# Cross attention of a two-layer decoder: projections and output product as three rounded products, their weights fetched and split piece by piece

## The reference

```python
q = (x @ Wq).reshape(B, Sq, 16, 128)          # x: 512 x 512,   Wq: 512 x 2048
k = (ctx @ Wk).reshape(B, Skv, 16, 128)       # ctx: 512 x 256, Wk: 256 x 2048
v = (ctx @ Wv).reshape(B, Skv, 16, 128)
q = rmsnorm(q, gq); k = rmsnorm(k, gk)
scores = einsum('bqhd,bkhd->bhqk', q, k) / sqrt(128)
out = einsum('bhqk,bkhd->bqhd', softmax(scores), v)
out = out.reshape(B, Sq, 2048) @ Wo           # Wo: 2048 x 512
```

## Time and profile before

| | us |
|---|---|
| median of 3 runs | 2998.81 (2998.12 to 3002.98) |
| profiled execution | 3006.79 |
| its span, first to last instruction | 3005.1 |
| TensorE busy | 2727.0, 91% |
| VectorE busy | 1975.9, 66% |
| ScalarE busy | 1100.2, 37% |
| GpSimd busy | 633.0, 21% |

### The profile page before, as it was taken

The page is one execution under the profiler, slowest core; times in us unless marked ns, Lnnn a source line. Parts: engine busy times, 40 slices in busy tenths (PEclk is TensorE's granted clock), DMA queues, the critical chain, the costliest instruction groups (busy, mean ns, idle before and its releaser), DMA issues.

```text
span 3005.1 us, 28723 instructions
## 1 busy us (share of the span) xinstructions
PE 2727.0 (91%) x8882; PEld 1493.1 (50%) x8882; DVE 1975.9 (66%) x3923; ACT 1100.2 (37%) x1999; POOL 633.0 (21%) x569
## 2 busy tenths in 40 slices
PE   6887887888869988899999999999999999899998
PEld 2333333333337845455545555455545555488886
DVE  3896996997996547688836787378826887323332
ACT  4335335335333322255514554155514454121111
POOL 0542543533520136411101110111101110000000
PEclk9998988998989989999999999999999999999999
DMA  3111111111130213200021001200011002400000
GB/s 118 49 56 44 63 43 54 60 49 50 61 114 29 77 43 139 80 15 18 15 58 51 18 15 31 79 18 15 19 58 49 17 15 80 141 7 28 29 15 14
DMA packets 67406, 145.34 MB, mean 48 GB/s; under 512 B 8115, under 2 KB 24755, under 8 KB 66230
## 3 DMA queue, kind: packets, MB, share of 16 engines
q1 hardware_dynamic: 58134, 111.40, 11.2%
q0 software_dynamic: 5472, 21.01, 1.8%
q10 hardware_dynamic: 3648, 11.08, 1.1%
HBM read 113.77 MB, written 29.69 MB: 48 GB/s over the span
## 4 chain that ended last, share of the span: by engine, by line
PE 64%; DVE 16%; issue 10%; POOL 5%; ACT 2%; DMA 1%; SPq 1%; DVEq 0%; POOLq 0%; ACTq 0%
PE bank L492 34%; PE bank L834 7%; POOL h L1603 3%; PE bank L789 3%; DVE h L1266 3%; PE bank L848 3%; PE bank L849 3%; PE bank L852 3%; DVE sm L1526 2%; DVE p L1537 1%; DVE val L1465 1%; PE bank L877 1%; PE bank L878 1%; PE bank L774 1%; PE bank L879 1%
## 5 line engine op out<-in xcount | busy, mean ns | idle before, releaser
L1603 POOL TENSOR_TENSOR h<-du,Bb 128x1024 f32<-128x1024 f32 x128 | 300.4, 2350 | 212.7 <-DVE h L1271 163.0
L1266 DVE TENSOR_TENSOR_SCAN h<-bank,h 128x512 f32<-128x512 f32 x256 | 297.8, 1203 | 33.6 <-ACT bank L967 18.3
L967 ACT ACTIVATE bank<-dt,A 128x512 f32<-128x512 f32 x256 | 174.9, 690 | 310.1 <-DVE h L1266 309.9
L1112 ACT ACTIVATE p<-bank,sm,rq 128x512 f32<-128x512 f32 x256 | 199.1, 778 | 210.1 <-DVE sm L1530 210.1
L492 PE MATMUL bank<-pT,v 128*128 128x512 f32 x512 | 234.7, 602 | 3.0 <-ACT pT L904 3.0
L834 PE MATMUL bank<-woh,oT 128*128 128x512 f32 x512 | 226.0, 603 | 10.8 <-DMA woh<-in_Wo 8.8
L492 PE MATMUL bank<-xT,wxq 128*128 128x512 f32 x512 | 230.6, 593 | 3.2 <-ACT xT L904 3.2
L1678 POOL TENSOR_TENSOR rq<-rq,mhalf 128x4 f32<-128x4 f32 x64 | 65.6, 1025 | 791.0 <-DVE rq L1517 791.0
L209 POOL TENSOR_SCALAR rstd<-mv 128x1 f32<-128x1 f32 x96 | 25.4, 265 | 979.8 <-DVE mv L203 979.8
L492 PE MATMUL bank<-kr,q 128*128 128x512 f32 x512 | 230.6, 593 | 0.0
L1526 DVE TENSOR_REDUCE sm<-bank 128x1 f32<-128x512 f32 x256 | 175.3, 685 | 33.9 <-PE bank L492 33.7
(11 more groups left out here) (203 smaller groups left out, 5109.9 us busy)
## 6 DMA issues: line engine op xcount, KB each, us to landing
Bb<-bc_dram SPq DMA_DIRECT2D x32, 512.0 KB, 3.6
Cb<-bc_dram SPq DMA_DIRECT2D x32, 512.0 KB, 3.8
x_dram<-xo POOLq DMA_DIRECT2D x16, 1024.0 KB, 4.7
xc<-x_dram SPq DMA_DIRECT2D x16, 1024.0 KB, 5.3
woh<-in_Wo SPq DMA_DIRECT2D x64, 256.0 KB, 2.7
idx<-in_idx SPq DMA_DIRECT2D x64, 129.0 KB, 2.1
w_dram<-val SPq DMA_DIRECT2D x64, 129.0 KB, 2.5
xc<-in_x SPq DMA_DIRECT2D x4, 1024.0 KB, 7.4
```

The costliest lines, as they stand in the source:

```text
L967: act.activation(bank[2 + n][:, :], dt[:, et, :], ACT.Exp, scale=A[:, et, 2 * w + n:2 * w + n + 1]).then_inc(dA_ready, 1)
L1112: act.activation(p4[:, t, :], bank[4 + t][:, :], ACT.Exp, bias=sm4[:, 4 + t:5 + t], scale=rq[:, hh % 2, 1, t:t + 1], accum_out=sm4[:, 8 + ...
L1266: dve.tensor_tensor_scan(h[:, s, n, :], bank[2 + n][:, :], h[:, s, n, :], 0.0, ALU.mult, ALU.add).then_inc(scanned, 1)
L1603: pool.tensor_tensor(h[:, U % HR, :, :], du[:, et:et + 1, :].to_broadcast([P, 2, S]), Bb[:, w % 2, :, :], ALU.mult).then_inc(dBu_ready, 1)
```

## The change

All four linear products of stage 3 (keys, values, queries, and the output product of sequences 0 to 2) become three rounded products each. The context, x, the weights and the attended values are split into hi and lo. ScalarE rounds; GpSimd subtracts for the three projection weights; VectorE subtracts for the context, x, the attended values and the `Wo` slices. The weights are no longer loaded whole: `Wq` comes per head (128 columns, two buffers), `Wk` and `Wv` per group of four heads (512 columns, one buffer each), again in each sequence. GpSimd's part of the stage is written out for every sequence instead of running in a loop. In stage 0 the keys take the same form as the queries (two Relu passes and an exponential on ScalarE, a plain sum of two SBUF tiles on VectorE), and `key_consumed` is gone. The last sequence keeps its output product in float32.

```diff
-    def key_consumed(j):
-        pe.wait_ge(qk_ready, START + after(c, KD + NT, KD + j + 1))
...
+    dst = qp[:, j, :] if j < KD else kp[:, j - KD, :]
+    dve.tensor_tensor(dst, er[:, j % 2, 0, :], er[:, j % 2, 1, :], ALU.add).then_inc(qk_ready, 1)
...
-    weights(3, wxq, io["Wq"]); weights(3, wxk, io["Wk"]); weights(3, wxv, io["Wv"])
+    load_ctx(0)
+    load_wxk(0)
+    load_wxv(0)
+    load_wxq(0)
+    load_wxq(1)
...
@@ SyncE, in each head @@
+    if after(c, XH, hh + 2) < B * XH:
+        load_wxq(after(c, XH, hh + 2))
+    if hh % 4 == 3 and after(c, GROUPS, hh // 4 + 2) < B * GROUPS:
+        load_wxv(after(c, GROUPS, hh // 4 + 2))
+        load_wxk(after(c, GROUPS, hh // 4 + 2))
...
@@ TensorE @@
     def queries(hh):
+        pe.wait_ge(wxq_split, START + after(c, XH, hh + 1))
+        pe.wait_ge(x3_split, START + after(c, KD, KD))
         d = bank4("q", hh)
-        group(d[:, :], [(wxq[:, k, hh * P:(hh + 1) * P], xT[:, k, :]) for k in range(KD)], a_full)
+        three4(d[:, :], [p for k in range(KD) for p in (
+            (wxq_hi[:, hh % 2, k, :], x_hi3[:, k, :]), (wxq_lo[:, hh % 2, k, :], x_hi3[:, k, :]),
+            (wxq_hi[:, hh % 2, k, :], x_lo3[:, k, :]))], a_full)
...
@@ output product, c < B - 1 @@
+    pe.wait_ge(o_split, START + after(c, XH, hh + 1))
+    for t in range(NT):
+        tt = slice(t * P, (t + 1) * P)
+        pe.matmul(bank[4 + t][:, :], o_hi3[:, hh % 2, tt], w_hi3[:, hh % 2, :], start=(hh == 0), stop=False)
+        pe.matmul(bank[4 + t][:, :], o_hi3[:, hh % 2, tt], w_lo3[:, hh % 2, :], start=False, stop=False)
+        m = pe.matmul(bank[4 + t][:, :], o_lo3[:, hh % 2, tt], w_hi3[:, hh % 2, :], start=False, stop=(hh == XH - 1))
...
@@ ScalarE, in each head, behind oT(hh-1) @@
+    if after(c, XH, hh + 2) < B * XH:
+        round_wxq(after(c, XH, hh + 2))
+    if hh % 4 == 0 and after(c, GROUPS, hh // 4 + 1) < B * GROUPS:
+        round_wxv(after(c, GROUPS, hh // 4 + 1))
+    if hh % 4 == 1 and after(c, GROUPS, hh // 4 + 1) < B * GROUPS:
+        round_wxk(after(c, GROUPS, hh // 4 + 1))
...
+    def round_out(hh):
+        act.wait_ge(wo_loaded[hh % 2], START + 16 * after(c, XH // 2, hh // 2 + 1))
+        if hh >= 2:
+            act.wait_ge(wo_used, START + after(c, XH - 1, hh - 1))
+        act.wait_ge(a_done, START + A0[3] + after(c, PER_A[3], TILES4["o", hh] + 1))
+        act.activation(o_hi3[:, hh % 2, :], oT[:, hh, :], ACT.Copy)
+        act.activation(w_hi3[:, hh % 2, :], woh[:, hh % 2, :], ACT.Copy).then_inc(o_rounded, 1)
...
@@ VectorE @@
+    def out_rest(hh):
+        dve.wait_ge(o_rounded, START + after(c, XH, hh + 1))
+        dve.tensor_tensor(o_lo3[:, hh % 2, :], oT[:, hh, :], o_hi3[:, hh % 2, :], ALU.subtract)
+        dve.tensor_tensor(w_lo3[:, hh % 2, :], woh[:, hh % 2, :], w_hi3[:, hh % 2, :], ALU.subtract).then_inc(o_split, 1)
...
     key_norms(0)
+    x3_rest()
     key_scale(0)
...
@@ at the end of head 12, c < B - 1 @@
+    ctx_rest(c + 1)
...
@@ GpSimd @@
+def wxq_rest(n):
+    pool.wait_ge(wxq_rounded, START + n + 1)
+    pool.tensor_tensor(wxq_lo[:, n % 2, :, :], wxq[:, n % 2, :, :], wxq_hi[:, n % 2, :, :], ALU.subtract).then_inc(wxq_split, 1)
```

More of the change, by code:

```diff
@@ L743, in bank4, with three4 @@
                             return bank[k % 3]
+                        def three4(dst, pairs, inc):
+                            for n, (l, r) in enumerate(pairs):
+                                m = pe.matmul(dst, l, r, start=(n == 0), stop=(n == len(pairs) - 1))
+                            m.then_inc(inc, 1)
                         def ready4(*name):
@@ L801, in _ @@
                         for k in range(KD):
+                            if k == 3:
+                                pe.wait_ge(x3_split, START + after(c, KD, 1))
                             d = bank4("x", k)
@@ L1117, in _ @@
                         for k in range(KD):
-                            bring(xT[:, k, :], got("x", k))
+                            bring(x_hi3[:, k, :], got("x", k))
                         queries(0)
@@ L1134, in _ @@
                                 keys(hh // 4 + 1)
+                            if hh == 12 and c + 1 < B:
+                                round_ctx(c + 1)
+                        if c < B - 1:
+                            round_out(0)
+                            round_out(1)
                         bring(oT[:, XH - 1, :], got("o", XH - 1))
+                        if c < B - 1:
+                            for hh in range(2, XH):
+                                round_out(hh)
             if stages >= 5:
@@ L1517, in query_mean, with ctx_rest, x3_rest @@
                             dve.tensor_scalar(rq[:, hh % 2, 0, :], bank[3][:, 0:4], 1.0 / XD, LN_EPS, ALU.mult, ALU.add).then_inc(rq_raw, 1)
+                        def ctx_rest(n):
+                            dve.wait_ge(ctx_rounded, START + n + 1)
+                            dve.tensor_tensor(ctx_lo[:, :, :], ctx4[:, :, :], ctx_hi[:, :, :], ALU.subtract).then_inc(ctx_split, 1)
+                        def x3_rest():
+                            for k in range(KD):
+                                dve.wait_ge(a_done, START + A0[3] + after(c, PER_A[3], TILES4["x", k] + 1))
+                                dve.tensor_tensor(x_lo3[:, k, :], bank[TILES4["x", k] % 3][:, :], x_hi3[:, k, :], ALU.subtract).then_inc(x3_split, 1)
+                        def out_rest(hh):
+                            dve.wait_ge(o_rounded, START + after(c, XH, hh + 1))
+                            dve.tensor_tensor(o_lo3[:, hh % 2, :], oT[:, hh, :], o_hi3[:, hh % 2, :], ALU.subtract)
+                            dve.tensor_tensor(w_lo3[:, hh % 2, :], woh[:, hh % 2, :], w_hi3[:, hh % 2, :], ALU.subtract).then_inc(o_split, 1)
+                        if c == 0:
+                            ctx_rest(0)
                         key_norms(0)
+                        x3_rest()
                         key_scale(0)
@@ L1544, in _ @@
                                 key_norms(hh // 4 + 1)
+                            if hh == 12 and c + 1 < B:
+                                ctx_rest(c + 1)
+                        if c < B - 1:
+                            for hh in range(XH):
+                                out_rest(hh)
                         if c == B - 1 and stages >= 5:
@@ L1663, in _ @@
                     continue
+                if n == 3:
+                    for c in range(B):
+                        cross(c)
+                    continue
                 with pool.Fori(0, B // 2) as i:
```

161 lines of the change are left out of this document (118 added, 43 removed).

## The result

The changed kernel takes 3006.4 us (median of 10 runs, 3002.7 to 3016.9) against 2998.15 us for the kernel before (10 runs, 2995.9 to 3003.0). The ratio is 1.0032, with a 95% interval from 1.0023 to 1.0040: slower by 0.3%, where 2961 us was forecast. The profiled execution took 3006.47 us with a span of 3004.8; that of before had taken 3006.79, by chance 8.6 above its own median, so the two traces are equally long and can be compared stretch by stretch. One stretch of a trace is good to a few us only: the same code behind the last head's first selection takes 467.3 to 472.5 us over the traces of this case.

The account below looks back on a forecast made before the run. TensorE was taken to lead in the groups, VectorE's look-up in the last four heads, TensorE alone in the output product. The terms summed to -38.1 us, giving 2961 us from the median 2998.81, range 2930 to 3002.

Parts of the forecast that it names:

- GpSimd against VectorE: Stage 3 heads: GpSimd's weight subtractions partly block VectorE, 2 us per group and 3 in the last four heads: +33 us.
- L1465 stretched at all: Sign of a wrong forecast: the look-up's eight selections, expected to be free, lengthen, so their window is no shelter.
- Rival 2: Stage 3: GpSimd blocks VectorE in full, +116, sum +45, 3044 us; sign turns at 61%; chance 0.1 for anything above break-even.
- Rival 4: VectorE bounds the groups too, which stay at 67.6 us; only the output product gains: 2996 us, chance 0.05.
- The groups: Stage 3, 12 groups of four heads: each takes 63.3 us instead of 67.6, together -51.6 us.
- The last four heads: End of each sequence: stay at VectorE's 13.29 us per head, plus ctx_rest in three sequences: +4.2 us.
- The output product: Three sequences: 45.6 us each, first product 1.1 later, so 8.5 less each: -25.5 us.
- The boundary: Between sequences, three times: VectorE's x parts eat the keys' and values' 2.65, about 0.9 stays: -2.7 us in all.
- The start of stage 3: First keys wait for the rests of context and keys, 1258.9 us at best instead of 1251.64: +6.5 us.
- Stage 0: Without key_consumed TensorE starts about 1.3 us earlier; between -2.1 and +2.3 per sequence, taken as -2 over four.
- The sum: All terms: -51.6 + 4.2 - 25.5 - 2.7 + 6.5 - 2 + 33 = -38.1 us.
- Rival 3: TensorE's granted clock drops to 1.2 GHz in places of stage 3: about +25, 2986 us, chance 0.1.

Follow-up runs that it names:

- experiment 7: Kernel before plus one GpSimd subtraction per head, the eight selections taking constants for their two table columns: 3114.2 us; with 128x1024 subtractions 3019.1 us, ratio 1.0074.
- experiment 5: Changed kernel with the three weights' subtractions cut to 4 columns per slice after the first ones, results wrong: 2931.7 us, ratio 0.9768.
- experiment 8: GpSimd subtraction moved right behind the head's inverse root, beside the row maxima: added to the kernel before 3005.9 us; in the changed kernel 2972.9 us.

## Why the prediction was wrong, point by point

- **The step that failed: GpSimd against VectorE, +33.** It assumed: "So they seem to read one port at the plain rate, as the scans do, and I expect them to be free." The selections were the worst hit of all, +86 us (258.0 against 171.6); "L1465 stretched at all" had been named as a sign of being wrong. The step compared 0.35 us with the masks' 0.25 at one length and took the difference for a plain pace. By the rows in experiment 7 it is a fixed part of some 120 ns. And the earlier trace rows held the counter-example: L1287 is itself a `tensor_scalar` with a column (in PSUM), and it was held. The look-up grew by 112 us, three quarters of the 151 that all 92 subtractions come to by the prediction's own lengths, and the kernel lost 75 (experiment 5): the term was 42 too small.
- **Rival 2** had the right mechanism and too high a time (3044): it put 116 on the path, and 75 fell there. That is 65%, just past its break-even of 61%.
- **Rival 4** foretold that a group stays at 67.6, and it did (68.2 against 67.9), but by the hold of rival 2 and not by VectorE's own work. Its sum is wrong: -38 without the groups' -51.6 is +13.5, not -3, so 3012 and not 2996.
- **The groups, -51.6**: measured +4.3. With the subtractions cut away it is 12 x (64.2 - 67.9) = -44, with them on VectorE -33. So the walk through the group was about right (64.2 against 63.3); what failed was the step above.
- **The last four heads, +4.2**: +28.3, of which +2.9 is left without the subtractions. VectorE has no slack there, as the earlier trace rows said, and each held microsecond counts fully: the look-ups there are 25.2 us longer than before, and the heads 25.4 longer than with the subtractions cut away.
- **The output product, -25.5**: -25.9 by itself. 45.4 to 48.4 a sequence against 45.6. Right.
- **The boundary, -2.7**: product and boundary together were to give -28.2 and gave -19.6; with the subtractions cut away -20.0. Over three boundaries the changed kernel's product starts 2.3 later and is 25.3 shorter. From the first keys to the first query it takes +0.2, and from there to the first selection +3.3. The waits for `x_lo` eat the matmuls' 2.65, as the prediction had read it:

```profile
PE bank L792 <- DVE x_lo L1638: 6.5, 4, 1.6
PE bank L867 <- DVE x_lo L1638: 6.2, 4, 1.9
```

  The +3.3 is TensorE's clock. In the kernel with the rests cut away, the queries behind the first of these boundaries run at a granted clock of 1.00 (2.4 GHz), those behind the third at 0.50 (1.2 GHz):

```profile
1575.00:1578.00 3.00, 2.97 (x14) 2.42 (x15) 2.50 (x4) 0.00 (x0) 0.13 (x1) 1.00 0.02 5
2216.00:2219.00 3.00, 3.00 (x8) 2.32 (x8) 2.33 (x4) 0.00 (x0) 0.00 (x0) 0.50 0.00 0
```

  From the first query to the first selection it takes 13.0 us at the first and 15.4 at the third, where the kernel before takes 13.7. The twelve query matmuls start 0.23 us apart in the one and 0.43 in the other, which is nearly the whole 2.4. In the changed kernel most of these matmuls start 0.43 apart at all three boundaries. So the forecast gain of 0.66 is there at full clock, and the low clock turns it into a loss of 1.7. TensorE stood for `x_lo` ahead of both; why the clock fell ahead of one alone no run shows.
- **The start of stage 3, +6.5**: +8.2 up to the first selection. About right.
- **Stage 0, -2**: -19 in the trace, -18.6 alone. I had seen both halves in the earlier trace rows, a wait of 12.72 and one of 2.15 behind it, and priced only TensorE's start. What the late TensorE did to the scans (11.2 us over four sequences) was in the waits, and I didn't add them up; the 6.8 us of the product I had not foreseen.
- **The sum again**, from the traces of before and of the kernel with the rests cut away: stage 0 -17.5, start +8.4, groups -44.3, last heads +2.9, product and boundaries -20.0, behind the last head +1.1. That is -69.4, and the spans are 3005.1 and 2935.6. The forecast had -71.1 there. So the errors in stage 0 (15 too little), groups (7 too much) and boundaries about cancel, which is luck, and 42 of the forecast's 45 us of error are the contention's.
- **Rival 3**, the clock: granted 0.95 in stage 3, against 0.99 before. With the rests cut away it is 0.98, with them on VectorE 0.97. It is lower where TensorE is idle longer (37 us of the stage before, 69, 81 and 109 in the order 0.98, 0.97, 0.95). At the boundaries its price can be read, as above; in the heads no run here separates it from that of the waits.

The Trainium skill (SBUF — State Buffer, "Who interferes with whom") holds that a VectorE instruction with at most one SBUF input, outside the two-port modes, does not contend with GpSimd. The selections with constants have one SBUF input and were held for up to 2300 ns, so by that rule they must run in a two-port mode. No row names the mode; that their time per element is half that of a subtraction (experiment 7) fits it, and the selections with columns share that pace. What the page says of two SBUF inputs agrees with the product of one column, held for 1.71 us.

## What to carry to other kernels

Before giving GpSimd work beside VectorE, list VectorE's instructions in that window by where their operands lie: in this kernel the maxima, which read only PSUM, went undisturbed, and 84 of 90 instructions of the look-up that began beside a subtraction waited for its end. Don't read a pace from one length: a fixed part looks like a slow pace, and two lengths of the same kind tell them apart. If VectorE itself would do the work in less time than GpSimd blocks (here 83 us against a look-up 112 us longer), keep it there. When one change bundles several edits, time each alone: here two of them together were worth 1.6%, and the third took it all back.

## What the hardware showed that I had not expected

- An instruction's size is no shelter: one of 128x1 elements, 159 ns alone, took 1.71 us beside a subtraction and 2133 ns at most.
- The hold goes both ways: GpSimd's 128x512 subtraction of Wq takes 1278 ns on average beside the maxima and 1421 beside the look-up.
- What is held runs on when the subtraction ends, and it has done part of its work by then. In the kernel before with the early subtraction (experiment 8) a squaring of two SBUF inputs (L1500, 691 ns alone) began at 1315.87, GpSimd's subtraction ended at 1315.12 + 1.26 = 1316.38, and the squaring took 1.06: 0.51 beside the subtraction and 0.55 behind it.
